# A graph layer with decaying neighbour weights: one-tile units at both ends, marks chosen per unit, differences over eight beats, counts between the products

## The reference

```python
h = relu(layernorm(x))                      # rows of 64, eps 1e-5
support = h @ weight
mask = (adj != 0)
rank = cumsum(mask, axis=1)                 # along the 4096 columns
deg = rank[:, -1:]
k = minimum(deg, 100)
pos = rank - (deg - k)
w = mask * where(pos > 0, 0.5 ** (k - pos), 0)
out = x + w @ support + bias
```

## Time and profile before

| | us |
|---|---|
| median of 3 runs | 245.06 (244.77 to 246.62) |
| the profiled execution's own time | 244.41 |
| its span, first to last instruction | 242.1 |
| busy in it: PE, DVE, ACT, POOL | 208.9, 206.9, 170.2, 31.3 |
| granted clock of PE, mean | 0.979 |

### The profile page before, as it was taken

The page is one execution under the profiler, slowest core; times in us unless marked ns, Lnnn a source line. Parts: engine busy times, 40 slices in busy tenths (PEclk is TensorE's granted clock), DMA queues, the critical chain, the costliest instruction groups (busy, mean ns, idle before and its releaser), DMA issues.

```text
span 242.1 us, 6387 instructions
## 1 busy us (share of the span) xinstructions
PE 208.9 (86%) x2816; PEld 203.0 (84%) x2816; DVE 206.9 (85%) x285; ACT 170.2 (70%) x302; POOL 31.3 (13%) x53
## 2 busy tenths in 40 slices
PE   0530766886999999999999999999999999999993
PEld 0530654776998999999999999999999999999982
DVE  0999979999999999999998999998999995526424
ACT  2411636856687888787888887888887888888640
POOL 8500000004001040104040104030000000000000
PEclk9995699999999999999999999999999999999999
DMA  7999999999999999999999999994000000000000
GB/s 204 191 217 217 195 214 215 215 217 215 217 217 215 218 215 216 218 213 220 214 218 214 218 215 212 214 204 106 0 14 3 11 3 14 0 14 7 6 14 22
DMA packets 7386, 36.11 MB, mean 149 GB/s; under 512 B 1088, under 2 KB 3136, under 8 KB 3136
## 3 DMA queue, kind: packets, MB, share of 16 engines
q0 software_dynamic: 4608, 33.56, 67.1%
q1 hardware_dynamic: 2448, 2.10, 3.1%
q10 hardware_dynamic: 304, 0.07, 0.1%
HBM read 68.22 MB, written 1.05 MB: 286 GB/s over the span
## 4 chain that ended last, share of the span: by engine, by line
PE 68%; DVE 21%; DMA 5%; issue 2%; ACT 1%; POOL 1%; POOLq 0%
PE acc L529 30%; PE chain L511 22%; PE chain L509 10%; DVE masks L292 8%; DMA adj_b<-in_adj 5%; DVE powers L322 3%; PE tot L475 2%; DVE powers L318 2%; DVE part L300 2%; PE chain L490 1%; PE chain L496 1%; DVE sums L310 1%; DVE support L385 1%; ACT powers L257 1%; DVE powers L380 1%
## 5 line engine op out<-in xcount | busy, mean ns | idle before, releaser
L257 ACT ACTIVATE powers<-chain 128x512 int16<-128x512 f32 (+1 forms) x272 | 156.8, 585 | 45.5 <-PE chain L511 27.6
L529 PE MATMUL acc<-support,powers 128*128 128x192 bf16 x1024 | 123.5, 246 | 4.1 <-DVE powers L322 4.0
L509 PE MATMUL chain<-diag_past,masks 128*128 128x128 bf16 x480 | 84.3, 225 | 5.8 <-ACT powers L257 5.7
L511 PE MATMUL chain<-diag_own,masks 128*128 128x128 bf16 x512 | 89.3, 227 | 0.0
L529 PEld LDWEIGHTS acc<-support,powers 128*128 128x128 bf16 x1024 | 82.8, 99 | 5.3 <-DVE powers L322 5.1
L509 PEld LDWEIGHTS chain<-diag_past,masks 128*128 128x128 fp8e3 x480 | 69.0, 148 | 8.7 <-ACT powers L257 8.2
L511 PE MATMUL chain<-diag_step,masks 128*128 128x128 bf16 x512 | 73.7, 226 | 0.0
L292 DVE TENSOR_SCALAR masks<-adj_b 128x4096 uint8<-128x4096 bf16 x32 | 72.6, 2286 | 0.3 <-DMA adj_b<-in_adj 0.2
L511 PEld LDWEIGHTS chain<-diag_own,masks 128*128 128x128 fp8e3 x512 | 68.7, 147 | 0.0
L511 PEld LDWEIGHTS chain<-diag_step,masks 128*128 128x128 fp8e3 x512 | 54.0, 148 | 0.0
L318 DVE TENSOR_SCALAR powers<-powers 128x1024 int16<-128x1024 int16 (+1 forms) x64 | 29.1, 455 | 22.7 <-ACT powers L257 22.7
(11 more groups left out here) (55 smaller groups left out, 88.5 us busy)
## 6 DMA issues: line engine op xcount, KB each, us to landing
adj_b<-in_adj POOLq DMA_DIRECT2D x32, 1024.0 KB, 22.0
x_sb<-in_x SPq DMA_DIRECT2D x1, 1024.0 KB, 5.0
out<-x_sb SPq DMA_DIRECT2D x16, 64.0 KB, 2.9
w<-in_L_gnn_weight ACTq DMA_DIRECT2D x2, 16.0 KB, 4.6
bias_b<-in_L_gnn_bias ACTq DMA_DIRECT2D x1, 32.0 KB, 4.2
```

The lines of the kernel that those rows point to most:

```text
L257: nc.scalar.activation(powers[:, c, b, at:].bitcast(i16), chain[c][:, at:], ACT.Relu, bias=(MAX_NEIGH + 1) * STEP).then_inc(powers_ready[c ...
L509: nc.tensor.matmul(chain[c][:, at:at + P], column(u, k, t + 1), diag_past[:, :], start=False, stop=False, skip_group_check=True)
L511: last = nc.tensor.matmul(chain[c][:, at:at + P], column(u, k, t), diag_own[:, :] if marked else diag_step[:, :], start=False, stop=True, ...
L529: last = nc.tensor.matmul(acc[a][:, k * 3 * D:(k + 1) * 3 * D], powers[:, c, s + 1 if marked else s, at:at + P], support[:, t, :, :].rearr ...
```

## The change

- **Units.** 18 units by a table SIZES: three of one tile, fourteen of two, one of one. The first and the last have four chains (CHAINS) of 8 steps, the others two of 16.
- **Marks.** MARKS says how many tiles of a unit are marked. Units 0 to 3 and 17 are marked throughout, 14 and 15 not at all, the rest one of two. A unit that is marked throughout has no differences, and its products wait for ACT alone (`before_products`).
- **Differences.** BATCH is 8: two batches a unit of 8 x 256 columns, or 8 x 512. The maximum (`floor`) goes to the front of a beat of DVE, the subtraction (`differ`) to its end. Products begin LAGS beats after the start: 11 for most, 14, 10 and 8 for the first three, 8 for the last.
- **Counts and products.** PE goes over the chains c, not the units. For each it waits for what both need, then issues product, count, product, count. The product may be that of the unit three before in the same bank's place.
- **Constant.** The 256-column matmul with `unmarked` is gone. The copy of the totals writes 127 partitions; partition 127 of `totals_t` holds the constant for the marked tiles.
- **Layer norm.** Both halves are normalized first, by DVE (`normalize`). The split in three parts is done in PSUM: PE multiplies, ACT copies a part, PE takes it off with `minus` (`take_off`), in the beats 5 to 11.
- **Loads.** `x` comes in two halves, `adj` as four loads, then POOL's memsets and subtraction, then the others. The squares lie in the seventh buffer of `adj_b`.

The core of it (the setting of tables and the loops):

```diff
-    K = 2
-    H = 2
-    MARKED = 2
-    BATCH = 4
-    BEHIND = 7
-    RING = 5
+    BATCH = 8
+    RING = 10
+    SIZES = [1, 1, 1, 2, 2, 2, 2, 2, 2, 2, 2, 2, 2, 2, 2, 2, 2, 1]
+    CHAINS = [4, 2, 2, 2, 2, 2, 2, 2, 2, 2, 2, 2, 2, 2, 2, 2, 2, 4]
+    MARKS = [1, 1, 1, 2, 1, 1, 1, 1, 1, 1, 1, 1, 1, 1, 0, 0, 1, 1]
+    STARTS = [0, 5, 10, 15, 22, 28, 33, 39, 45, 50, 56, 62, 67, 73, 79, 84, 90, 96]
+    LAGS = [14, 10, 8, 11, 11, 11, 11, 11, 11, 11, 11, 11, 11, 11, 11, 11, 11, 8]
...
-                nc.tensor.matmul(chain[c][:, 0:MARKED * P], unmarked[:, :], ones[:, :],
-                                 start=False, stop=False, skip_group_check=True)
...
-                for u in range(NU):
-                    b = g - start(u)
-                    if u and b == -2:
-                        turn_totals(u)
-                    if b == 0:
-                        base(u)
-                    if 0 < b < BEATS:
-                        count(u, b - 1)
-                    if 0 <= b - BEHIND < STEPS:
-                        product(u, b - BEHIND)
+                for c in range(FLIGHT):
+
+                    u = max((v for v in range(c, NU, FLIGHT) if STARTS[v] <= g <= STARTS[v] + STEPS[v]), default=None)
+                    vs = [v for v in range(c, NU, FLIGHT) if 0 <= g - STARTS[v] - LAGS[v] < STEPS[v]]
...
+                    for v in vs:
+                        before_products(v, g - STARTS[v] - LAGS[v])
+                    if u is not None:
+                        counted(u, g - STARTS[u] - 1)
+                    for i in range(4):
+                        for v in vs:
+                            if i < SIZES[v] * CHAINS[v]:
+                                last = product(v, g - STARTS[v] - LAGS[v], i // CHAINS[v], i % CHAINS[v])
...
+                        if u is not None and i < SIZES[u] * CHAINS[u]:
+                            last = count(u, g - STARTS[u] - 1, i // CHAINS[u], i % CHAINS[u])
+                            if i + 1 == SIZES[u] * CHAINS[u]:
+                                last.then_inc(chain_ready[c], 1)
```

The take-off of a part in PSUM, and the two halves of what was `differences`:

```diff
+            def take_off(i, s, ready):
+
+                pe.wait_ge(ready, i + 1)
+                t = 8 * BLOCKS[i]
+                nc.tensor.matmul(split[i % 2][:, :].rearrange("p (t d) -> p t d", d=D), minus[:, :],
+                                 support[:, t:t + 8, s, :], start=False, stop=True,
+                                 skip_group_check=True).then_inc(split_ready, 1)
...
+                bits = powers[:, c, first:last + 1, plain(u)].bitcast(i16)
+                nc.vector.tensor_scalar(bits, bits, STEP, None, ALU.max).then_inc(floored[c], 1)
...
+                before = powers[:, c, BATCH * j:BATCH * j + BATCH, plain(u)]
+                after = powers[:, c, BATCH * j + 1:BATCH * j + BATCH + 1, plain(u)]
+                nc.vector.tensor_tensor(before, before, after, ALU.subtract).then_inc(weights_ready[c], 1)
```

More of the change, by code:

```diff
@@ L115, in gnn_decay_kernel @@
         tot = pb("tot", [P, 512], fp32)
[L116 to L119 removed]
+        turned = (acc[0], acc[1])
+        split = (acc[2], acc[3])
+        x_loaded = [sem(f"x_loaded{f}") for f in range(2)]
         bias_loaded = sem("bias_loaded")
@@ L232, in high_part @@
[L232 to L240, removed]
+                nc.scalar.activation(half_of(sq, f), half_of(cen, f), ACT.Square).then_inc(sq_ready, 1)
@@ L252, in weigh @@
                 c = u % FLIGHT
[L253 to L257, removed]
+                if b == 0 and MARKS[u] == SIZES[u]:
+                    return
+                act.wait_ge(chain_ready[c], taken_until(u) + b + 1 - (MARKS[u] == SIZES[u]))
@@ new lines, in _ @@
+                if g == 10:
+                    part(2, 1, middle_ready)
+                    part(3, 1, middle_ready)
+                if g == 11:
+                    part(2, 2, low_ready)
+                    part(3, 2, low_ready)
+                for c in range(FLIGHT):
+                    for u in range(c, NU, FLIGHT):
+                        if u and g == STARTS[u] - 1:
+                            turn_out(u)
+                        if 0 <= g - STARTS[u] <= STEPS[u]:
+                            weigh(u, g - STARTS[u])
@@ L432, in _ @@
+            mask(3)
+            add_bias(0)
+            add_bias(1)
+            dve.wait_ge(xb_ready, 2)
             for g in range(SLOTS + 4):
                 for u in range(NU):
-                    if BATCH < g - start(u) <= BEATS and (g - start(u) - 1) % BATCH == 0:
-                        differences(u, (g - start(u) - 1) // BATCH - 1)
-                later_half(g)
+                    if MARKS[u] < SIZES[u] and g - STARTS[u] in range(BATCH + 1, STEPS[u] + 2, BATCH):
+                        floor(u, (g - STARTS[u] - 1) // BATCH - 1)
@@ new lines, in base, with count @@
+                if MARKS[u] < SIZES[u]:
+                    last.then_inc(chain_ready[c], 1)
+            def count(u, s, k, h):
+                c = u % FLIGHT
+                t = T - 1 - STEPS[u] * h - s
+                at = (k * CHAINS[u] + h) * P
+                marked = k < MARKS[u]
+                n = FIRST[u] + k
+                if s and marked:
+                    nc.tensor.matmul(chain[c][:, at:at + P], column(n, t + 1), diag_past[:, :],
+                                     start=False, stop=False, skip_group_check=True)
+                return nc.tensor.matmul(chain[c][:, at:at + P], column(n, t),
+                                        diag_own[:, :] if marked else diag_step[:, :],
+                                        start=False, stop=True, skip_group_check=True)
```

610 lines of the change are left out of this document (327 added, 283 removed).

## The result

| us | before | after |
|---|---|---|
| median | 244.92 | 232.66 (232.57 to 234.71) |
| profiled execution, span | 244.41, 242.1 | 232.57, 230.8 |
| PE, DVE busy | 208.9, 206.9 | 206.5, 188.7 |

The ratio is 0.951, 95% interval 0.944 to 0.958. The forecast was 236.0.

A forecast was written before the change was run, and what follows sets the result against it. PE was taken to bound from 79 to 227 us, DVE from 34 to 79. Beat 15 at 46.5, work 181.7, waits 1.5 and end 3.3 gave a 233.0 span; with 2.3 and 0.65 outside it, 236.0 us, range 231 to 242.

The forecast's parts named there:

- beat 15 at 46.5: Start: the beat from which PE's remaining work was summed, forecast at 46.5 us, bounds 43 and 52.
- rival of a start no earlier: Start: ACT's support steps wait in line, beats 5 to 11 cost 3.1 us each, not 2.35; 242.0 us, chance 0.12.
- Beats 5 to 11: Start: beats carrying the support, 16.5 us of ACT steps and round trips to PE.
- PE's work: PE from beat 15 on: products, counts and other matmuls priced by their neighbours, sum 181.7 us.
- rival of alternating for nothing: PE's blocks: counts take 0.0618 us wherever they stand; 3.6 us more, 239.6 us, chance 0.12.
- check of its prices on the kernel before: Kernel before, from unit 6's base: 138.0 us priced against 138.8 to the last product, so prices hold within 1%.
- Waits: PE from beat 15 on: waits for ACT and for differences, together 1.5 us, bounds 0 and 6.
- ACT's loop: Blocks through ACT: slack falls from 0.8 to 0.46 us; as a rival it becomes the bound, 244.0 us, chance 0.09.
- the worst crowd: DVE: a floor, an addition, a first halving and a difference take 3.1 us, fitting a window of 4.5.
- rival of late differences: DVE one mask behind: 5.3 us against 4.5, PE stops 0.8 at each of 26 batches; 257 us, chance 0.07.
- 2 us of slack for tile 10: Loads: tile 10, the tightest, lands at 60.9 us and is wanted at beat 26, at 63.1.
- The end: Last beats: PE's work is unbroken, about 3 us of waits go; 3.3 us stay behind the last product.

The follow-up runs named there:

- soon3: marks3 with the subtraction of units 0 to 3 right behind its maximum on DVE, ahead of the same beat's mask; 231.91 us.
- start_two: The changed kernel with two-tile units from the start and the two one-tile units at the end; 238.56 us.
- soon23: soon3 with unit 2 unmarked too, its products 11 beats behind its start instead of 8; 234.48 us.
- before_alternating: The kernel before with only the alternation of products and counts added; 247.67 us, ratio 1.010.
- marks3: The changed kernel with one tile of unit 3 unmarked; 235.22 us.
- blocks: The changed kernel with four products in a row and then the counts of the same chain, instead of alternating; 237.26 us.
- end_two: The changed kernel with a two-tile unit, one tile marked, alone at the end, and two one-tile units at the start; 235.50 us.

## Why the prediction was right

- **The sum.** Measured less forecast, by its own terms: beat 15 at 46.5, measured 42.7 (-3.8); from there to the last product 183.2, measured 184.5 (+1.3); behind it 3.3 and 3.6 (+0.3); outside the span 2.3 and 1.8 (-0.5); median over the profiled execution 0.65 and 0.1 (-0.6). Together -3.3. The mechanism was right, the size was off in the start; 232.66 lies 1.7 above the lower bound of the range.
- **The start.** First totals 16.98 (16.6), counts 20.05 (19.7), 0.35 late. The rival of a start no earlier falls with beat 15 at 42.7. The mis-sized terms follow. Beats 1 to 4 took 5.0 us, not 6.4: PE begins the transposes of beat 5 at 25.06, right behind the last count, without another turn through ACT, and two of the beats ran at the upper level of the clock, 1.42 and 1.40 us each. In the profile of soon3, without that stretch, they take 1.76 and 1.77, so the forecast's lower level was right for most profiles and its 1.6 a little short. Beats 5 to 11 took 15.2 us, not 16.5. The number and kind of ACT's steps were right (30 in the row below; the terms of the prediction add up to 16.7, not 16.5), but ACT is busy 13.2 us with them and not 14.6, since steps that stand back to back overlap by about 0.1 us; its idle time, 2.0, is that of the seven round trips, 2.1. Beats 12 to 14 took 2.5, not 3.9: 1.3 was the loop of a lone chain of 512 columns, these are two chains of 256. That the one-tile start matters is shown by start_two, 5.9 us.

```profile
25.06:40.23 15.17, 13.94 (x127) 11.68 (x125) 14.41 (x13) 13.21 (x30) 1.61 (x4) 0.92 1.03 210
```

- **PE's work.** The pitches held (0.0559, 0.0644, 0.0825), and alternating is worth 3.4 us in the stretch where it works, against 3.6: the rival of alternating for nothing falls. The prediction's check of its prices on the kernel before set the work of the whole of beat 38, which begins at 98.58, against a length from 100.00; like with like leaves 2.2 us and not 0.8, and lone beats and late differences at the end are about as long. Its reason for the place's effect, that a strided column comes in behind the longer product, is not shown; the runs show only that the place of a count decides. "PE bounds from beat 15" was a little early: beats 16 to 19 have 0.1 to 0.3 us of waits each, and in soon23 they do not follow PE's work.
- **Waits.** Forecast 1.5 us; the stretch is 2.8 longer than the work as the prediction summed it. ACT's loop does not bound: beats with three chains are as long as PE's work. before_alternating shows what the same order costs where one chain is alone, 0.27 us a beat.
- **Differences.** PE waits for them 0.3 us in all. But the margin was less than the forecast's: 0.6 us at a batch behind a mask, where 4.5 against 3.1 left 1.4. The sum of the worst crowd had left out the mask (2.2 us) that can stand ahead of the maximum. The rival of late differences was right in its mechanism and stood one beat away.
- **DVE in the first 60 us** was called no hindrance, since there are no differences before beat 31. That was the reason, and marks3 shows its worth: 2.6 us. The 2 us of slack for tile 10 were not there: tiles 1 to 10 come 5.05 us apart and not 4.9, the beats come earlier than forecast, and DVE waits 2.6, 2.5 and 2.9 us for tiles 6, 8 and 10 (mask of tile 10 at 62.35, its beat at 60.6). PE does not see it, for the same reason.
- **The end.** Forecast about 3 us of waits gone, measured 2.9 in waits.

The parts that were undone singly, 5.9 for the start, 4.6 for alternating and 2.7 for the end, sum to 13.2 against a gain of 12.3. That is near, but not a proof of each: the second holds some 1 us that is not PE's order, the third moves the start as well. What the dropped matmul of the constant, the support's new place and the order by chains each give was not tried alone.

## What to carry to other kernels

Price a saturated engine by the distance of starts for each kind of neighbour, not by a mean duration: here the priced work was 181.7 of 184.5 us, the rest waits. An order that saves time per instruction can lengthen a loop through another engine, so look at what now lies inside the loop where few chains are in flight. Before work is moved to an engine with spare time, see what stands in front of it in its queue, and whether that waits for a transfer.

## What the runs showed of the hardware

- A 128-column matmul whose weights are a column of `masks` (one byte in 32) takes 55.9 ns as the first behind a product of 192 columns, 64.4 as the second and 61 to 63.5 from then on. With `sums` as weights (fp8 too, one byte in 4 or 8) it takes 55.8 wherever it stands. The weight loads differ in the profile as well: 143 to 148 ns (medians) for the first, 98 for the second and for the bf16 `powers`. The two kinds differ in their moving operand and their bank too, and the stride alone was not varied. Why the second costs most was not tried.
- The granted clock at the start is not the same from run to run. In the profiles of the change and of soon23 counts are 0.06 apart from 21.5 to 24 us and 0.11 from 24.2 to 27.5; in those of blocks and soon3 they are 0.107 apart from the first up to 29.5 and 25.7 us. The figure reads 1.00 in the last two all the while (22 to 29 us in blocks), so where it reads 1.00 in the first microseconds look at the spacing.
- The clock can fall once more in the middle: to 0.50 from 68 to 71 us in end_two, behind a stop of 2.44 us. A stop of 2.37 us in marks3 was not followed by a fall.
